# The first guess of three reciprocal roots moves from VectorE to GpSimd, as a power and one Newton step

## The reference, cut to what matters

```python
xn = layernorm(x)
# edges: gate = sigmoid(silu(rbf @ W1 + b1) @ W2 + b2); aggr = segment_sum(gate * xn[src], dst)
# nodes: xn + silu([xn, aggr] @ U1 + c1) @ U2 + c2
q, k, v = heads(xn @ wq.T), heads(xn @ wk.T), heads(xn @ wv.T)   # 4 heads of 64
k, v = layer_norm(k) * kg + kb, layer_norm(v) * vg + vb          # over the 64 of a head
mix = (q @ (k^T v / S)) @ wo.T + bo
x = x + gnn + mix
x = x + experts(layernorm(x))     # top 2 of 16 experts, hidden 512
```

## Time and profile before

| | |
|---|---|
| time, median of 3 runs | 1199.55 us (1198.32 to 1203.38) |
| span of the profiled execution | 1109.2 us; its time with what lies around the span is not listed apart |
| median less span | 90.35 us |
| TensorE busy | 1053.5 us, 95% of the span |
| VectorE busy | 887.2 us, 80% |
| ScalarE busy | 691.9 us, 62% |
| GpSimd busy | 747.1 us, 67% |

### The profile page before, as it was taken

One profiled execution on the slowest core, in us unless ns is written; L12 is line 12 of the kernel. 1 busy time (PEld: TensorE's weight loads), 2 busy tenths in 40 slices (PEclk: granted clock), 3 DMA queues, 4 the chain that ended last, 5 costly groups with the idle time before them and its releaser, 6 DMA issues.

```text
span 1109.2 us, 23680 instructions
## 1 busy us (share of the span) xinstructions
PE 1053.5 (95%) x7990; PEld 993.3 (90%) x7990; DVE 887.2 (80%) x1409; ACT 691.9 (62%) x1075; POOL 747.1 (67%) x703
## 2 busy tenths in 40 slices
PE   4897999999999999999999999999799999999995
PEld 2465899999999999999999989997599999999995
DVE  7877888888999888888899972488777777777773
ACT  2562667766666666666666643664467777777663
POOL 5447777777777777777777756540147777777764
PEclk9998999999999999999999998999899999999998
DMA  7211445545444544444455420222458988988972
GB/s 243 77 55 37 137 142 143 143 144 140 143 141 137 146 140 141 142 142 142 142 143 143 144 60 25 71 86 56 153 171 232 229 224 228 225 229 211 240 192 22
DMA packets 118495, 159.74 MB, mean 144 GB/s; under 512 B 20536, under 2 KB 91020, under 8 KB 118412
## 3 DMA queue, kind: packets, MB, share of 16 engines
q0 software_dynamic: 31104, 66.28, 26.0%
q1 hardware_dynamic: 86748, 91.60, 25.3%
q10 hardware_dynamic: 560, 0.79, 0.3%
HBM read 142.42 MB, written 18.17 MB: 145 GB/s over the span
## 4 chain that ended last, share of the span: by engine, by line
PE 87%; DVE 7%; issue 2%; ACT 2%; DMA 1%; DVEq 0%; POOLq 0%; POOL 0%; SPq 0%; ACTq 0%
PE ps L1595 25%; PE ps L1786 16%; PE ps L1606 15%; PE ps L1549 8%; PE ps L1798 8%; PE ps L1650 4%; PE ps L1523 2%; PE ps L1662 2%; PE ps L1675 2%; PE ps L1725 1%; PE ps L1773 1%; DVE st L979 1%; PE ps L1532 1%; PE ps L1533 1%; PE ps L1516 1%
## 5 line engine op out<-in xcount | busy, mean ns | idle before, releaser
L1595 PE MATMUL ps<-fr 128*128 128x256 f32 x2352 | 306.6, 287 | 3.2 <-DVE fr L1041 3.2
L1595 PEld LDWEIGHTS ps<-fr 128*128 128x128 f32 x2352 | 288.9, 192 | 4.1 <-DVE fr L1041 4.0
L590 POOL DMA_INDIRECT big<-xn_rows,srcs x200 | 219.6, 1098 | 61.3 <-issue 61.3
L590 POOL DMA_INDIRECT hgx<-xn_rows,srcs x192 | 210.5, 1096 | 58.5 <-issue 58.5
L742 ACT ACTIVATE h1f<-ps,b 128x512 f32<-128x512 f32 x196 | 124.2, 684 | 167.3 <-PE ps L1549 166.4
L1606 PEld LDWEIGHTS ps<-oh,big 128*128 128x128 f32 x1568 | 190.7, 192 | 8.7 <-DVE big L1177 0.5
L1786 PE MATMUL ps<-fr 128*128 128x256 f32 x1536 | 191.5, 285 | 2.7 <-issue 1.4
L1786 PEld LDWEIGHTS ps<-fr 128*128 128x128 f32 x1536 | 188.2, 193 | 3.2 <-issue 1.7
L1606 PE MATMUL ps<-oh,big 128*128 128x96 f32 x1568 | 189.0, 274 | 0.4 <-DVE big L1186 0.4
L1041 DVE TENSOR_TENSOR fr<-h1f,fr 128x1024 fp32r<-128x1024 f32 x98 | 120.1, 1225 | 51.8 <-ACT fr L745 51.7
L662 POOL DMA_INDIRECT out<-xnT,idx x64 | 117.9, 1842 | 50.3 <-issue 35.3
(11 more groups left out here) (219 smaller groups left out, 1418.5 us busy)
## 6 DMA issues: line engine op xcount, KB each, us to landing
big<-in_w SPq DMA_DIRECT2D x128, 256.0 KB, 4.3
rbf<-in_rbf SPq DMA_DIRECT2D x98, 256.0 KB, 2.9
big<-in_w SPq DMA_DIRECT2D x32, 512.0 KB, 4.3
xn_rows<-xn SPq DMA_DIRECT2D x26, 128.0 KB, 2.6
big<-xn_rows,srcs POOLq DMA_INDIRECT x200, 3.2
xn_rows<-hgx SPq DMA_DIRECT2D x24, 128.0 KB, 2.2
hgx<-xn_rows,srcs POOLq DMA_INDIRECT x192, 3.2
x_nodes<-in_x SPq DMA_DIRECT2D x2, 768.0 KB, 9.2
```

Of the source, the lines that this page charges most:

```text
L590: pool.indirect_dma_start(hg[i % HB][:, s, :], None, xn_d[:, :], bass.IndirectOffsetOnAxis(srcs[:, col:col + 1], 0))\
L1595: last = mm(ps[:, 2 + 4 * p + s // 2, (s % 2) * D:(s % 2 + 1) * D], h1s[p][a][:, c, s * P:(s + 1) * P], W2s[b][:, c, :], start=c == 0 and ...
```

## The change

On VectorE, `kv_seed` now ends after adding epsilon, and announces the variance on a new semaphore. GpSimd raises the variances of the batch to the power -0.5 (`guess`, one `tensor_tensor` with a column of -0.5), and announces that. One Newton step stands in the loop turn after the seed; it waits for the power, and then announces the batch, one turn earlier than before. GpSimd's `guess` for a batch stands ahead of `scale_v` of tiles 0, 4, 10, 14 and 17. `layer_stats` of the last chunk (5 values a partition) does the same; its power is the last thing in GpSimd's node phase. The first norm and the other chunks of the last norm stay as they are.

```diff
+            pool.memset(minus_half[:, :], -0.5)
...
+            def guess(k, y, v):
+                pool.wait_ge(s_var, k + 1)
+                pool.tensor_tensor(y, v, minus_half[:, 0:1].to_broadcast(list(v.shape)), ALU.pow).then_inc(s_root, 1)
...
             for t in range(NT):
+                for k, (a, b) in enumerate(zip(KVCUT, KVCUT[1:])):
+                    if t == max(b + 1 - KLAG, 0):
+                        guess(k, kvr[:, a * 8:b * 8], r_v[:, 0:(b - a) * 8])
                 scale_v(t)
                 add_biases(t)
...
             silu_low(NB - 1, 0, 1)
+            guess(len(KVCUT) - 1, rstd[:, CHUNKS[-1][0]:NT], v_c[:, 0:NT - CHUNKS[-1][0]])
...
-            def layer_stats(t, n):
+            def layer_stats(t, n, last=False):
                 q = slice(t, t + n)
                 v = v_c[:, 0:n]
                 link(dve.tensor_scalar(v, mv[:, q, 1], EPS, None, ALU.add))
+                if last:
+                    y, a, b = rstd[:, q], v_a[:, 0:n], v_b[:, 0:n]
+                    dve.sem_inc(s_var, 1)
+                    dve.wait_ge(s_root, len(KVCUT))
+                    link(dve.tensor_tensor(a, y, y, ALU.mult))
+                    link(dve.scalar_tensor_tensor(b, a, -0.5, v, ALU.mult, ALU.mult))
+                    link(dve.scalar_tensor_tensor(y, b, 1.5, y, ALU.add, ALU.mult))
+                    return
                 rsqrt(rstd[:, q], v, v_a[:, 0:n], v_b[:, 0:n])
...
                 link(dve.tensor_scalar(v, ssq[:, a * 8:b * 8], EPS, None, ALU.add))
-                link(dve.tensor_scalar(u.bitcast(i32), v.bitcast(i32), 1, None, ALU.arith_shift_right))
-                link(dve.tensor_scalar(y.bitcast(i32), u.bitcast(i32), -1.0, MAGIC, ALU.mult, ALU.add))
-            def kv_step(k, i):
+                dve.sem_inc(s_var, 1)
+            def kv_step(k):
                 a, b, y, v, u, w = kv_batch(k)
+                dve.wait_ge(s_root, k + 1)
                 link(dve.tensor_tensor(u, y, y, ALU.mult))
                 link(dve.scalar_tensor_tensor(w, u, -0.5, v, ALU.mult, ALU.mult))
                 link(dve.scalar_tensor_tensor(y, w, 1.5, y, ALU.add, ALU.mult))
-                if i == 2:
-                    dve.sem_inc(s_kvr, b - a)
+                dve.sem_inc(s_kvr, b - a)
...
-                for i in range(3):
-                    if t - 1 - i in KVCUT[1:]:
-                        kv_step(KVCUT.index(t - 1 - i) - 1, i)
+                if t - 2 in KVCUT[1:]:
+                    kv_step(KVCUT.index(t - 2) - 1)
...
-                        layer_stats(t0, end - t0)
+                        layer_stats(t0, end - t0, end == NT)
```

More of the change, by code:

```diff
@@ L202, in gps_layer @@
         left_p = sb("left_p", [P, 1])
+        minus_half = sb("minus_half", [P, 1])
         flag = sb("flag", [P, 1], i32)
@@ L299, in gps_layer @@
         s_kvr = sem("kv_rstd_made")
+        s_var = sem("variances_made")
+        s_root = sem("roots_guessed")
         s_kh = sem("k_scaled")
```

## The result

In the first comparison the changed kernel took 1218.95 us (median of four runs, 1209.64 to 1223.80) and the kernel before 1201.47 us (four runs, 1198.32 to 1208.40): a ratio of 1.0139, 95% interval 1.0078 to 1.0200, which is 17 us more. The forecast was 1196.3 us, the range 1194.0 to 1207.0. Later, beside each other on two other chips, the ratio was 1.0263 (1.0243 to 1.0283) and 1.0277 (1.0261 to 1.0294), 29 and 30 us more. Every ratio and its interval leave out slow executions (those over 1.5% above the same kernel's fastest), while the medians given with them do not, so that a ratio need not be that of the two medians.

A forecast was written before the change was run, and what follows sets the result against it. TensorE was taken as the bound, 87% of the chain; gains of 1.4 (batch 0), 1.0 (batch 4) and 0.9 us (last norm) sum to 3.3 us, from 1199.55 to 1196.3 us, range 1194.0 to 1207.0.

The forecast's parts named there:

- the price of a power: GpSimd's power, estimated as twelve passes: 1.2 us for 48 elements, 0.9 for 32, 0.73 for 24, 0.35 for 5.
- ceiling: Dearest price assumed for GpSimd's power, twenty passes: 2.0 us for 48 elements; 2.0 us gained in all, 1197.5 us.
- The first rival: Slow power makes GpSimd the bound in batches 1 to 3 from about 50 ns an element; 9.9 us slower at 100; chance 0.2.
- The third rival: TensorE runs at half clock after idle times; two further slow stretches cost 3 us, giving 1199.3 us; chance 0.15.
- the floor price: Cheapest price assumed for GpSimd's power, one pass of 0.3 us whatever the batch; 4.4 us gained in all, 1195.2 us.
- Batch 0: First key and value statistics, 38 to 43 us: 1.4 us gained, 1.9 at the cheapest power, 0.65 at the dearest.
- Batches 1 to 3: TensorE without a gap from 43.84 to 86 us: nothing gained, nothing lost while a power takes up to 2.2 us.
- Batch 4: Last key and value statistics, 88 to 99 us: 1.0 us gained, 1.4 at the cheapest power, 0.6 at the dearest.
- The norm: Last norm, 757 to 767 us: eight VectorE instructions go, 0.9 us gained, bounds 1.1 and 0.75; last logits could be late.
- Second rival: First power waits for a code load of 1.28 us: 2.0 us gained, 1197.6 us; chance 0.1; a 6 us load gives 1202.3.
- These don't change: The 90.35 us between the profiled span of 1109.2 us and the time of 1199.55 us were taken as fixed.
- The shared port: VectorE and GpSimd exclude each other for a whole instruction; row-scaling holds batch 0's power, its gain about 0.3 us less.

The follow-up runs named there:

- e_keep: Changed kernel with unused products in TensorE's queue ahead of each batch's first product; 1213.26 us, ratio 1.0197 against the kernel before.
- e_b1: Kernel before with only batch 1 started by a power, at the change's place; 1209.17 us, ratio 1.0147 against the kernel before.
- e_cheap: Changed kernel with GpSimd's power replaced by a multiply and add, the guess's shift staying on VectorE; 1108.79 us, ratio 1.0004 against the kernel before.
- e_norm: Kernel before with only the last chunk of the last norm started by a power; ratio 0.9999 against the kernel before.
- e_late: Kernel before with powers in batches 1 to 3, two tiles later in GpSimd's queue than in the change; 1214.84 us, ratio 1.0191.
- e_early: Kernel before with tiles 0 to 2 by an early power, tiles 3 to 5 guessed later; 1198.34 us, ratio 1.0042; again without pauses (e_early2) 1109.47 us, 1.0007.
- e_threes: Kernel before with powers of three tiles, four in the last, some four tiles ahead, for all tiles but 3 to 5; 1116.78 us, ratio 1.0075.

## Why the prediction was wrong

**The step that failed is the price of a power**: "0.25 us + 20 ns an element", with "ceiling: twenty passes, 36 ns" (20 times 1.7 is 34). It measured 0.4 us + 159 ns. The working took the count of passes from nothing that a row shows, and then called the resulting 36 ns a ceiling. Everything downstream went by it: "past 2.2 us every further microsecond is paid in each batch" was right in kind (the waits put the mark at 2.7 us, 8.0 less 5.3), and the power took 8.0.

**The first rival was the case.** It turned at 50 ns an element and was worked out at 100 ns. With the measured prices in the same formulas: batch 0 loses 2.4 + (8.0 - 5.05) = 5.4, batches 1 and 2 lose 8.0 - 2.2 = 5.8 each, batch 3 loses 1.5 + (5.4 - 3.45) = 3.5, batch 4 loses 0.9 + (4.2 - 2.65) = 2.4: 22.9 us. The waits summed to 19.9, with the mark at 2.7 and not 2.2 us; the first key product came 5.2 us late (49.05 for 43.84), by the formula 5.4; and e_keep, which has hardly more than the waits, lost 22 in the stage. It got a chance of 0.2 because an ordinary pass costs 1.7 ns an element, which says nothing on a power.

**What was missing beside the price** is the clock. The third rival had the mechanism ("time at half clock costs half its length") but only as something that might take a gain back. It comes with four of the five gaps that the first rival makes (not with the 2.94 us one), so the two belonged in one sum: 6 to 7 us of 28 (e_keep), 2.8 us for one gap of 5.4 (e_b1).

**The places of the gain, read from e_cheap.** Its instruction of 0.23 us is below the floor price of 0.3, so it is to be held against the floor's 4.4 us, and not against the 3.3 of powers of 1.2 us. **Batch 0**: the floor said 1.9 us. The first key product came 1.7 us earlier, at 42.22 and not 43.90 (its wait fell from 1.71 to 0.60), and e_cheap keeps the shift, 0.2 us, on VectorE, so this bears out. **Batches 1 to 3** cost nothing, as said. **Batch 4**: 0.9 us (2.6 us at the edge phase less 1.7 from batch 0) where the floor said 1.4; the scatter of the start is 0.7. **The norm**: the floor said 1.1 us. The chain shrank by 1.06, but only 0.2 us was kept at the step on the logits, since the last logits, which I had named as "the next thing that could be late" and charged 0.07 us, were late by 0.8. With the power the chain shrank by 0.3 us and not 0.9, from the price alone; the changed kernel kept that (9.60 us for 9.89), e_norm did not. So where a cheap instruction should have gained 4.4 us, 3.15 were there at the gathering for the experts, and no gain shows in the medians.

**Second rival, code that must be loaded**: refuted. The first power began 0.13 us after its variance (38.39 for 38.07 + 0.19) and took 8.05 us, the next two 8.02 and 8.01. The Trainium skill (GPSIMD Engine Reference, section on instruction dispatch) has about 6 us for a first call; no run here shows it.

**"These don't change", of 90.35 us between span and time**: wrong as a picture. Where span and time of one execution are both known they lie 1.8 to 3.1 us apart, with pauses (1211.1 and 1214.16 in the changed kernel's) and without (1106.1 and 1108.04). So the 90 us were not around the span: the profiled execution had no pauses, and the timed ones, by their times, had them inside theirs. The forecast of a difference does not suffer, but a range of 13 us does, where runs of one kernel spread over 32 us (1179.36 to 1211.78).

**The shared port**: by the Trainium skill (SBUF — State Buffer, section on who interferes with whom) a VectorE instruction with two SBUF inputs contends, for an exclusive lock, with a GpSimd one that reads SBUF. Taken for the whole instruction, as the prediction took it, that would have VectorE's scaling at 58.81 stand until 66.74. It took 0.46 us, against 0.42 with GpSimd idle. The measurement decides: a power does not hold VectorE off. Beside GpSimd's plain scalings it was slowed: the first instruction of the Newton step took 0.61 us at 66.77, with a value scaling beginning at 66.70, and 0.21 us at 46.47, with GpSimd idle. The prediction's 0.49 against 0.19 us was of that kind.

## What to carry to other kernels

A function on an engine whose rows show only plain passes has no ceiling from those rows; either run it once by itself or let the rival with the dear price carry as much chance as the cheap one. Compare the length of the longest single instruction on one engine with the lead that its queue has over the engine it feeds: 8 us stalled TensorE at both places tried, with leads of 2.7 and 4.3 us, and pieces of 4.2 us, set further ahead of their use, cost 1.1 us of waits in five. And price a new wait of TensorE of the length seen here, over 5 us, at about one and a half times its length, since the products behind it run at the half clock for a while: 8.2 us for 5.4 in e_b1, 28 for 20 in the change.

## What was not expected of the hardware

- A power on GpSimd: 8.03, 5.43, 4.17 and 1.20 us for 48, 32, 24 and 5 elements a partition, and 8.05 us for 48 in e_b1, on the chip with pauses. In e_late they were longer, 8.24 and 8.20 us for 48 and 5.61 for 32, and 4.25 us for 24 as the first of e_early, e_early2 and e_threes.
- VectorE ran at its usual pace beside it, also with two SBUF inputs: 0.46, 0.43, 0.43 and 0.43 us for the key scalings that fell into four of the powers:

```profile
84.42 0.43 DVE L1047 TENSOR_TENSOR oh<-big,kvr 128x256 f32<-128x256 f32 x1 [0.60 <-DVE hgx L1030]
102.79 0.43 DVE L1047 TENSOR_TENSOR oh<-big,kvr 128x256 f32<-128x256 f32 x1 [0.23 <-DVE hgx L1030]
113.97 0.43 DVE L1047 TENSOR_TENSOR oh<-big,kvr 128x256 f32<-128x256 f32 x1 [0.23 <-DVE hgx L1030]
```

  Beside a plain pass of GpSimd the same instruction took twice that: 0.85 us at 77.70, where GpSimd added biases for 0.73 us from 77.54.
- Five traces, the changed kernel's first and four of experiments on one chip, have pauses of all engines between the first edge product and the last norm, with waits of ScalarE of up to 11.9 us in the first (13.4 in e_b1) and 77 us lost in all there; eight traces on two other chips have none. By the times of the kernel before, it has them where they occur. What makes them stays open.
